# A graph network on one core: the one-hot of destinations moved from VectorE to ScalarE, with two orders of waiting changed

## The reference

```python
h = x
for _ in range(2):
    edge_input = concat([h[ei], h[ej], edge_attr], axis=-1)     # 128 + 128 + 32
    m_ij = relu(edge_input @ We1 + be1) @ We2 + be2
    h = h + segment_sum(m_ij, ej, N)
x = layernorm(x + h + bias)
# convolution: deg = segment_sum(edge_weight, dst) + 1, symmetric normalisation
x = layernorm(relu(segment_sum(h[src] * norm, dst) + bias1) + x)
```

## Time and profile before

| | |
|---|---|
| time, median of 3 runs | 2493.58 us (2489.06 to 2494.75) |
| time of the profiled execution | 2492.94 us |
| its span, first to last instruction | 2491.1 us |
| pass 0, first to last gather | 54.4 to 985.0 us |
| pass 1, first to last gather | 1037.4 to 1975.8 us |
| busy PE / DVE / ACT / POOL | 2223.8 / 1524.0 / 470.5 / 1747.1 us |
| mean granted clock of TensorE, share of full speed | 0.929 |

### The profile page before, as it was taken

One profiled execution on the slowest core, in us unless ns is written; L12 is line 12 of the kernel. 1 busy time (PEld: TensorE's weight loads), 2 busy tenths in 40 slices (PEclk: granted clock), 3 DMA queues, 4 the chain that ended last, 5 costly groups with the idle time before them and its releaser, 6 DMA issues.

```text
span 2491.1 us, 49611 instructions
## 1 busy us (share of the span) xinstructions
PE 2223.8 (89%) x15066; PEld 1727.0 (69%) x15066; DVE 1524.0 (61%) x4032; ACT 470.5 (19%) x1057; POOL 1747.1 (70%) x1765
## 2 busy tenths in 40 slices
PE   2799999999999997899999999999998769999996
PEld 2576666666666666666666666666666669999995
DVE  2766666666666663465555555555554378777785
ACT  1211111111111111211111111111111133222322
POOL 2577777777777776377777777777777557777673
PEclk8899999999999995699999999999999579999998
DMA  5333333333333343333333333333333221111111
GB/s 125 81 100 99 100 99 100 99 100 99 100 100 100 99 99 97 87 81 99 100 98 99 99 95 98 98 98 99 100 98 92 66 64 50 50 50 50 46 49 50
DMA packets 156484, 218.67 MB, mean 88 GB/s; under 512 B 74232, under 2 KB 107887, under 8 KB 156276
## 3 DMA queue, kind: packets, MB, share of 16 engines
q0 software_dynamic: 56000, 114.80, 18.4%
q1 hardware_dynamic: 93236, 98.88, 14.7%
q10 hardware_dynamic: 7168, 4.09, 0.6%
HBM read 207.48 MB, written 10.12 MB: 87 GB/s over the span
## 4 chain that ended last, share of the span: by engine, by line
POOL 44%; issue 30%; PE 18%; DVE 3%; DMA 3%; POOLq 0%; ACT 0%; SPq 0%; DVEq 0%; ACTq 0%
POOL gat L523 44%; PE ps L708 6%; PE ps L699 6%; PE ps L593 3%; DMA gat<-dst_row 1%; PE ps L782 1%; DMA cbase_dram<-cint 1%; DMA gat<-z_dram,idx 1%; PE ps L778 1%; PE ps L651 1%; PE ps L611 1%; DVE node_a L1191 1%; DVE node_b L1097 0%; PE ps L627 0%; DVE node_b L1171 0%
## 5 line engine op out<-in xcount | busy, mean ns | idle before, releaser
L523 POOL DMA_INDIRECT gat<-p_dram,idx x1422 | 1418.2, 997 | 508.0 <-issue 450.3
L651 PE MATMUL ps<-node_a,x 128*128 128x512 bf16 x2400 | 739.6, 391 | 14.0 <-DVE node_a L1191 14.0
L593 PE MATMUL ps<-hot,msg 128*128 128x64 f32 x3232 | 425.4, 288 | 76.5 <-ACT msg L887 52.8
L1191 DVE TENSOR_SCALAR node_a<-ps,row_id 128x512 bf16<-128x512 f16 x1200 | 484.6, 467 | 8.4 <-PE ps L651 7.2
L593 PEld LDWEIGHTS ps<-hot,msg 128*128 128x128 f32 x3232 | 399.3, 201 | 97.8 <-ACT msg L887 63.0
L651 PE MATMUL ps<-node_a,adj 128*128 128x512 bf16 x1200 | 467.0, 389 | 0.0
L1153 DVE TENSOR_SCALAR lhs<-dbc,base_p 64x1024 f32<-64x1024 int32 x202 | 155.2, 768 | 477.2 <-DMA dbc<-dst_row 477.2
L583 PEld LDWEIGHTS ps<-rhs,lhs 96*128 96x128 f32 x3232 | 411.2, 200 | 44.1 <-DVE lhs L1153 15.6
L523 POOL DMA_INDIRECT gat<-z_dram,idx x328 | 318.9, 972 | 161.1 <-issue 98.4
L583 PE MATMUL ps<-rhs,lhs 96*128 96x128 f32 x3232 | 415.4, 284 | 14.6 <-DVE lhs L1153 10.8
L651 PEld LDWEIGHTS ps<-node_a,x 128*128 128x128 bf16 x2400 | 241.4, 104 | 269.0 <-issue 28.5
(11 more groups left out here) (146 smaller groups left out, 1650.2 us busy)
## 6 DMA issues: line engine op xcount, KB each, us to landing
dbc<-dst_row SPq DMA_DIRECT2D x202, 256.0 KB
lhs<-eaT SPq DMA_DIRECT2D x202, 128.0 KB
gat<-p_dram,idx POOLq DMA_INDIRECT x1422
rhs<-q_dram SPq DMA_DIRECT2D x202, 32.0 KB
gat<-z_dram,idx POOLq DMA_INDIRECT x328
idx<-src_g SPq DMA_DIRECT2D x243, 4.0 KB
p_dram<-node_a ACTq DMA_DIRECT2D x12, 256.0 KB, 3.4
q_dram<-node_b SPq DMA_DIRECT2D x12, 256.0 KB, 3.3
```

The lines of the kernel that those rows point to most:

```text
L523: return pool.indirect_dma_start(out=out_, out_offset=None, in_=table, in_offset=bass.IndirectOffsetOnAxis(ap=index, axis=0))
L593: last = nc.tensor.matmul(ps_agg(s), (msg if p < 2 else gat)[s][:, c, :], hot[s][:, c, (0 if p < 2 else 1), :], start=(c == 0), stop=(c == ...
L651: mm = nc.tensor.matmul(ps_own, p_part[k][:, t, :], shot[j % 2][:, t - t0, :, :].rearrange("p j e -> p (j e)"), start=(t == 0 and k == 0), ...
L1191: last = V.tensor_scalar(shot[j % 2][:, t - t0, :, :].rearrange("p j e -> p (j e)"), ps_ids, row_id[:, t:t + 1], None, ALU.is_equal)
```

## The change

The one-hot of destinations is made by ACT in two activations, |base - dbc| and then relu(1 - that), both into `lhs`, with a semaphore between them; DVE's `one_hots` goes. ACT makes group 0's behind the casts of `table_parts`, and group g+1's at the front of `relu(g)`. In PE's `sums` the tally products stand ahead of the wait for the relu, and the message sums of the first half wait for the first half's relu alone. In SP's `load` the destinations' DMA moves to the front, ahead of the wait for gathered rows and of the indices' DMA.

```diff
                         if old:
+                            sp.wait_ge(oht_made, nth(p, g) - 1)
+                        row = dst_row[bass.ds(g * GE, GE)].rearrange("(a n) -> a n", a=1)
+                        sp.dma_start(dbc[s][:, :], row.to_broadcast([W, GE])).then_inc(dbc_in[s], 16)
+                        if old:
                             if first:
                                 sp.wait_ge(rows_in[s][1], 16 * p * TAILS[s])
                             else:
...
-                        if old:
-                            sp.wait_ge(oht_made, nth(p, g) - 1)
-                        row = dst_row[bass.ds(g * GE, GE)].rearrange("(a n) -> a n", a=1)
-                        sp.dma_start(dbc[s][:, :], row.to_broadcast([W, GE])).then_inc(dbc_in[s], 16)
...
                     def sums(g, s):
                         n = nth(p, g)
-                        pe.wait_ge(relu_done, 2 * n + 2)
+                        if again(p, g):
+                            pe.wait_ge(agg_added, n - 1)
                         if p == 0:
                             pe.wait_ge(hotw_made, g + 1)
+                            tally_products(s)
                         else:
                             pe.wait_ge(hot_made, n + 1)
-                        if again(p, g):
-                            pe.wait_ge(agg_added, n - 1)
-                        scatter_products(p, s).then_inc(scat_mm, 1)
+                        pe.wait_ge(relu_done, 2 * n + 1)
+                        sum_products(p, s, 0, HALF)
+                        pe.wait_ge(relu_done, 2 * n + 2)
+                        sum_products(p, s, HALF, CH).then_inc(scat_mm, 1)
...
+                        def one_hots(g, s, k):
+                            n = nth(p, g)
+                            act.wait_ge(dbc_in[s], 16 * used(p, s, k))
+                            if again(p, g):
+                                act.wait_ge(pre_mm, 2 * (n - 1))
+                            nc.scalar.activation(lhs[s][0:W, :], dbc[s][:, :], ACT.Abs,
+                                                 bias=base_p[0:W, bass.ds(g, 1)], scale=-1.0).then_inc(away_made, 1)
+                            act.wait_ge(away_made, n + 1)
+                            nc.scalar.activation(lhs[s][0:W, :], lhs[s][0:W, :], ACT.Relu, bias=1.0, scale=-1.0
+                                                 ).then_inc(oht_made, 1)
+
                         def relu(g, s, k, j, q):
+                            if type(g) is not int or g < NG - 1:
+                                one_hots(g + 1, 1 - s, k + s)
...
+                        act.wait_ge(rel_ready, 2)
+                        one_hots(0, 0, 1)
                         groups(act, relu)
...
             def fast_steps(eng, scatter_hots, table_parts, vector_step, add_window, p):
-                one_hots(0, 0, 1)
                 scatter_hots(0, 0)
...
-                        if more:
-                            one_hots(g + 1, 1 - s, k + s)
```

More of the change, by code:

```diff
@@ L230, in build @@
         passed = sem("passed")
+        away_made = sem("away_made")
         oht_made = sem("oht_made")
@@ L585, in pre_products, with tally_products, sum_products @@
                 return last
[L587 to L591, removed]
+            def tally_products(s):
                 for c in range(CH):
+                    nc.tensor.matmul(ps_cw(s), tally[s][:, c, :], hot_bf(s)[:, c, :],
+                                     start=(c == 0), stop=(c == CH - 1))
+            def sum_products(p, s, c0, c1):
+                for c in range(c0, c1):
                     last = nc.tensor.matmul(ps_agg(s), (msg if p < 2 else gat)[s][:, c, :],
@@ L595, in scatter_products @@
                 return last
+            def scatter_products(p, s):
+                if p == 0:
+                    tally_products(s)
+                return sum_products(p, s, 0, CH)
             for p in range(3):
@@ L1067, in join, with fast_steps @@
                 V.tensor_tensor(dinv[:, :], dtmp[:, :], dmask[:, :], ALU.mult).then_inc(dchain, 1)
-            def fast_steps(eng, one_hots, scatter_hots, table_parts, vector_step, add_window, p):
-                one_hots(0, 0, 1)
+            def fast_steps(eng, scatter_hots, table_parts, vector_step, add_window, p):
                 scatter_hots(0, 0)
@@ L1146, in add_window @@
                         V.tensor_tensor(a, a, ps_agg(s), ALU.add).then_inc(agg_added, 1)
[L1148 to L1154, removed]
                     def scatter_hots(g, s):
@@ L1303, in _ @@
                     if p < 2:
-                        fast_steps(dve, one_hots, scatter_hots, table_parts, vector_step, add_window, p)
+                        fast_steps(dve, scatter_hots, table_parts, vector_step, add_window, p)
                     V.memset(scratch[:, :], 0.0).then_inc(agg_clear, 1)
```

## The result

The changed kernel takes 2447.86 us (median of 5 runs, 2440.10 to 2450.16), the kernel before 2491.92 (5 runs, 2489.06 to 2494.75): ratio 0.9818, 95% interval 0.9804 to 0.9833. That is 44.1 us less, where the sum said 43.2. The profiled execution took 2445.97 us, its span is 2443.8.

The account below looks back on a forecast made before the run. POOL's gathers were taken to bound passes 0 and 1. Savings of 36.6 (compare's stalls), 4.3 (ends) and 2.3 us (starts) sum to 43.2, from 2492.94 to 2449.7, say 2450 us; range 2424 to 2478.

Parts of the forecast that it names:

- The compare's stalls: Passes 0 and 1: 173 gathers held up behind VectorE's compare for the destinations' one-hot; moving it off saves 36.6 us.
- the other one-hot: VectorE's one-hot that PE scatters with, in passes 0 and 1: stalls of 21.6 us in 51 gathers, left unchanged.
- rival 1: Passes 0 and 1: the scatter one-hot starts behind the gather in pass 1; up to 21.6 us more saved, 2428; chance 0.18.
- rival 2: Passes 0 and 1: later landings shift VectorE instructions into the next gather; 10 to 30 us given back, 2460 to 2480; chance 0.13.
- rival 4: Passes 0 and 1: the scatter one-hot always starts ahead of the gather, 151 more steps stall; +74 us, 2524; chance 0.04.
- The starts: Beginnings of passes 0 and 1: PE's own part comes earlier and at a quicker rate in pass 0; 2.3 us saved, pass 1 nothing.
- The ends: Ends of passes 0 and 1: the tally and half the sums run before the last half lands; 4.3 us saved.
- ScalarE's time: Two activations per step on ACT, 2.06 us, fit within its 7.49 us of idle ahead of the relu; no cost.

Follow-up runs that it names:

- e4: The changed kernel with a 128 x 2048 compare, SBUF to SBUF, added on VectorE in each step of passes 0 and 1: 2556.07 us, ratio 1.0216.
- e5: The changed kernel with a reduction over 128 x 1280 float32 added on VectorE in each step of passes 0 and 1: 2457.75 us, ratio 0.9823.
- e1: The kernel before with only the destinations' one-hot moved to ScalarE, the orders of SP's `load` and PE's `sums` as before: 2449.82 us, ratio 0.9841.
- e7: The changed kernel run again without alteration, in a later set on another chip number: 2466.26 us, ratio 0.9855 to the kernel before.
- e8: The changed kernel with one further 64 x 1024 activation on ScalarE in each step: 2449.10 us, ratio 0.9840.
- e9: The changed kernel with four further 64 x 1024 activations on ScalarE in each step: 2458.74 us, ratio 0.9879.
- the second and third set: The runs e4 to e7 and the runs e8 and e9, each set with its own run of the kernel before: 2500.5 and 2486.7 us.
- e3: The kernel before with only PE's order changed (tally ahead, sums by halves): 2486.69 us, ratio 0.9983.
- e2: The kernel before with the new orders of SP's `load` and PE's `sums`, the compare still on VectorE: 2467.70 us, ratio 0.9912.
- e6: The changed kernel with the scatter one-hot's row of 64 numbers read from PSUM in passes 0 and 1: 2429.87 us, ratio 0.9718.

## Why the prediction was right

**The compare's stalls, 36.6 us.** Right in mechanism, and in size by the count: no gather ends behind a compare now, and the time inside the passes fell as the gathers did. e4 and e5 show that it is the kind of instruction and not VectorE's time, e1 that the move to ScalarE alone brings the gain. What the forecast left unchanged was not unchanged: the gathers of the two stretches became 42.5 us shorter (17.75 + 24.75), 5.9 more than 36.6, mostly because the other one-hot held up 29 gathers of pass 1 in place of 40. That is a part of rival 1, in this trace; in e7's the same kernel held up 70, which is the way of rivals 2 and 4. Its stalls (16.9 and 36.4 us in passes 0 and 1) account for the difference between the gathers of the two traces (1367.8 and 1386.9 us). The forecast left this term at 21.6 us; in the traces of the changed kernel and of its variants with both inputs in SBUF and no lock added (e1, e5, e8, e9) it lies between 10.0 (e1) and 36.4. Why the place of the one-hot against the gathers differs from one set to the next was not tried. That the chip makes it is not shown either: the second and third set ran on a chip of the same number, and the kernel before took 2500.5 us in one and 2486.7 in the other.

**The starts, 2.3 us.** 3.0 us in pass 0 (3.5 from its first gather, which came 0.5 later) and 0.4 lost in pass 1: 2.6, so the direction was right and the size close. Of the 3.0, PE's earlier own part brought 1.2, where 1.7 was forecast, and its quicker rate 1.8, where up to 1.7 was thought possible and about 0.6 taken.

**The ends, 4.3 us.** 2.26 + 1.68 = 3.9 in the profile, 3.7 in e3's time.

**ScalarE's time, no cost.** Right, with more room than the forecast saw: four further activations in each step, past PE's need, did not slow the gathers' pace. The two activations take 1.136 and 1.057 us, where 1.03 each was worked out from the nearest rows; the Trainium skill's page "ScalarE: Activation LUTs", section "What ACT_TABLE_LOAD costs", has the formula behind the estimate of 1.13 and 1.04 us, and the trace agrees. The Trainium skill's rule on that page, section "Rules for kernel authors", to run relu and the like on VectorE and not on ScalarE holds for the instructions here (2.19 us for two against 0.77) and not for this kernel.

**What cancelled.** The profiled execution fell by 47.0 us (2492.94 to 2445.97), 3.8 more than the sum; the medians by 44.1. That this lies within a microsecond or so of 43.2 is partly luck: the shorter stalls of the other one-hot gave 5 us more than forecast here and pass 2 took some back, and in e7's set the same change brought 34.2 us (2500.46 to 2466.26). The part behind pass 1's last gather grew by 0.5 us although its sums end 1.7 us earlier, so pass 2, which the change does not touch, took some 2 us more. L1072's stalls there rose from 4.3 to 7.3 us; whether that is the cause was not tried.

## What to carry to other kernels

Where GpSimd's indirect DMAs set the pace, look at the gathers whose duration stands out from the rest and at what VectorE did when they started: a common end, here 0.82 us behind one line, names the culprit. Such an instruction costs what it holds up, not its own duration, so take it to ScalarE, give it an input from PSUM, or use a form that holds up no gather, as the reduction of e5; VectorE's idle time is no evidence that it is harmless. Stalls that depend on 0.05 us of place came to 16.9 us in one trace of the same kernel and 36.4 in another, so compare variants within one set of runs, and count the stalls of every instruction again behind a change, those that it does not touch too.

## What the hardware showed that was not expected

A two-input tensor_tensor with both inputs in SBUF holds up a gather by up to 0.5 us (1.46 against 0.94 us), and with one input in PSUM it does not, in the same place. The Trainium skill, page "SBUF — State Buffer", section "Who interferes with whom", says of such an instruction that it contends with GpSimd's reads, which fits, and infers that the generation of descriptors is free of it. An indirect gather as a whole is not free of it, as the 70 gathers of e7 and their absence in e6 show. It also reads its indices from `idx` in SBUF, so the rule on reads may cover it, and no run tells which part of the gather was held up; the prediction's remark that the other one-hot's stalls would need another cause by that page does not follow.

A gather can be held up in two places: it ends either 0.82 us or 0.12 to 0.13 us behind the instruction that held it (e2's 1505.41 and 1505.53 is of the second kind; in the kernel before it was 144 and 29 behind the compare). What a gather does at these two places was not tried.
